# First attention of a Perceiver kernel: maxima and partial sums carried by transfers, divided by groups of four head pairs

## The reference

```
q = layernorm(x) @ Wq + bq            # 16 heads of width 16, scaled by 16 ** -0.5
k = ctx @ Wk + bk;  v = ctx @ Wv + bv # 2 batches x 4096 keys
o[h] = softmax(q[h] @ k[h].T) @ v[h]  # 32 (batch, head) products of 256 x 4096
x = x + concat(o) @ Wo + bo
```

## Time and profile before

| | |
|---|---|
| median of 3 runs | 1099.63 us (1094.17 to 1102.38) |
| profiled execution | 1102.66 us, its span 1101.4 us |
| first attention | 137.5 to 537.4 us of the span |
| TensorE busy over the span | 946.6 us (86%) |
| VectorE busy over the span | 822.6 us (75%) |
| ScalarE busy over the span | 650.5 us (59%) |
| GpSimd busy over the span | 299.6 us (27%) |
| mean granted clock of TensorE | 0.91 |

### The profile page before, as it was taken

One profiled execution on the slowest core, in us unless ns is written; L12 is line 12 of the kernel. 1 busy time (PEld: TensorE's weight loads), 2 busy tenths in 40 slices (PEclk: granted clock), 3 DMA queues, 4 the chain that ended last, 5 costly groups with the idle time before them and its releaser, 6 DMA issues. The chain is left out here.

```text
span 1101.4 us, 20954 instructions
## 1 busy us (share of the span) xinstructions
PE 946.6 (86%) x7732; PEld 589.9 (54%) x7732; DVE 822.6 (75%) x1712; ACT 650.5 (59%) x1045; POOL 299.6 (27%) x332
## 2 busy tenths in 40 slices
PE   6997859999999999998688996667887778799697
PEld 5886724444444444444365884643455556635455
DVE  5775777999999999992245987998877776278347
ACT  4442304888887878787354544249999999301212
POOL 1000088889800000000120552005555543000001
PEclk9998955999999999999799998776789999898989
DMA  6868651223323223310312216520165225770000
GB/s 215 307 226 281 243 143 39 76 76 80 82 76 81 74 75 82 82 45 1 76 43 87 79 37 160 132 64 1 43 167 152 58 58 171 217 203 8 0 0 20
DMA packets 99320, 111.83 MB, mean 102 GB/s; under 512 B 26658, under 2 KB 75730, under 8 KB 99218
## 3 DMA queue, kind: packets, MB, share of 16 engines
q1 hardware_dynamic: 98578, 109.89, 33.9%
q10 hardware_dynamic: 640, 0.59, 0.2%
HBM read 80.95 MB, written 29.43 MB: 100 GB/s over the span
## 5 line engine op out<-in xcount | busy, mean ns | idle before, releaser
L852 ACT ACTIVATE pT<-bank 128x512 f32<-128x512 f32 x512 | 278.4, 597 | 99.3 <-PE bank L769 78.7
L874 DVE TENSOR_REDUCE rmax<-bank 128x2 f32<-128x1024 f32 x256 | 307.3, 1223 | 32.3 <-PE bank L737 31.3
L781 PE MATMUL bank<-pT,V 128*17 128x256 f32 x2048 | 163.6, 392 | 4.7 <-ACT oT L858 4.6
L1755 PE MATMUL bank<-K1s,qs 97*128 97x512 f32 x256 | 112.7, 544 | 34.4 <-ACT work L1879 14.2
L769 PEld LDWEIGHTS bank<-qs,ks 49*128 49x128 f32 x1024 | 78.9, 189 | 114.9 <-ACT pT L852 101.3
L769 PE MATMUL bank<-qs,ks 49*128 49x256 f32 x1024 | 131.7, 336 | 2.3 <-ACT pT L852 0.5
L737 PE MATMUL bank<-ks,qs 49*128 49x512 f32 x512 | 111.9, 432 | 16.6 <-DMA ks<-k_parts_d 9.4
L2044 POOL TENSOR_TENSOR total<-total,work 128x1024 f32<-128x1024 f32 x40 | 94.9, 2379 | 32.9 <-ACT work L1879 32.0
L1755 PEld LDWEIGHTS bank<-K1s,qs 97*128 97x128 f32 x256 | 53.2, 219 | 51.8 <-issue 36.9
L1939 DVE MAX8 cand<-work 128x8 f32<-128x128 f32 x384 | 76.4, 277 | 0.0
L781 PEld LDWEIGHTS bank<-pT,V 128*17 128x17 f32 x2048 | 34.6, 95 | 64.3 <-ACT pT L852 41.7
(11 more groups left out here) (468 smaller groups left out, 1807.4 us busy)
## 6 DMA issues: line engine op xcount, KB each, us to landing
k_parts_d<-kparts SPq DMA_DIRECT2D x48, 512.0 KB
ks<-k_parts_d SPq DMA_DIRECT2D x381, 64.0 KB, 2.2
K1s<-k_parts_d SPq DMA_DIRECT2D x96, 128.0 KB
cn<-in_ctx SPq DMA_DIRECT2D x32, 384.0 KB, 3.5
cx<-in_ctx SPq DMA_DIRECT2D x16, 384.0 KB, 5.2
w<-in_L_ffn_w SPq DMA_DIRECT2D x32, 128.0 KB, 2.4
w2e<-in_L_ffn_w SPq DMA_DIRECT2D x16, 128.0 KB, 3.0
W<-in_L_xattn_W SPq DMA_DIRECT2D x2, 1024.0 KB, 7.8
```

The source lines that it names most:

```text
L781: t = pe.matmul(bank[32 * c:32 * c + VW, 7, a * S:(a + 1) * S], V[:, b * NCH + 4 * g + c, h, :], pT[:, (at + 2 * (c // 2) + a) % 8, c % 2 ...
L852: p_made.up(act.activation(pT[:, at % 8, :], bank[:, 4 + at % 3, :], ACT.Exp))
L874: max_read.up(dve.tensor_reduce(rmax[p % 2][:, :, qt, c], bank[:, b0:b0 + 2, :], AX.X, ALU.max))
L1755: m = pe.matmul(bank[:, b0 + c, :], qs1[0:NROW1, b * H1 + h, q], K1s[h][0:NROW1, keys], start=True, stop=(what == "new"))
```

## The change

The negated maxima no longer pass through TensorE: `move_rows(p)` on SP sends `nmax` (now 128 x 2 x 2) by four transfers of 128 elements into the row `MAX_ROW` of `qs`, and `scores(p, 0)` waits for these (`rows_in`). The sums no longer pass through TensorE either, but for the last pair: `move_parts(p)` on SP sends the four groups of `oT` by eight transfers into `parts` (the room of `xn`) and their sums into `den8`. `add_parts(k)` on GpSimd, behind its powers, adds the four parts of four pairs at once, VectorE takes the reciprocals of their sums in four pieces (`turn_den`), one after each of the maxima in steps 12 to 15 of pairs 4, 8 and 12 (`DEN_AT`), and `spread_den(k)` on SP spreads these by way of DRAM to `den16`; GpSimd multiplies. The last group holds three pairs, and pair 15 is added up by `add_quarters` at the end and divided by `divide_last`. The order of channels changes with it (the two heads of a pair are interleaved), so that `wo` is loaded in nine transfers instead of two, and the queries' high rows are interleaved so that a head's keys come in two transfers instead of three.

```diff
-    def steps_of(m, u):
-        return [(m, u)] + [(m - 1, "rows")] * (u == 0 and m > 0)
...
     def ahead(p, j):
         m, u = p + 1 + (j + LEAD) // 16, (j + LEAD) % 16
-        return steps_of(m, u) if m < NP_ else [(NP_ - 1, "rows")] * (m == NP_ and u == 0)
-
-    def beside(p, j):
-        return ahead(p, j) + [(p - 1, "sums")] * (j == 4 and p > 0)
-
-    passing = [what for u in range(16) for what in steps_of(0, u)]
-    passing += [what for u in range(LEAD) for what in steps_of(1, u)]
+        return [(m, u)] * (m < NP_)
+
+    passing = [(0, u) for u in range(16)] + [(1, u) for u in range(LEAD)]
+    DEN_AT = {}
     for p in range(NP_):
         for j in range(16):
-            passing += beside(p, j)
-    passing += [(NP_ - 1, "sums")]
+            passing += ahead(p, j)
+            if p % PG == 0 and p and j >= 12:
+                DEN_AT[len(passing) - 1] = (p // PG - 1, j - 12)
     place = {what: at for at, what in enumerate(passing)}
...
         powers_made.up(pool.tensor_scalar(Bp[1][:, :, :, :], Bp[1][:, :, :, :], -1.0, 0.0, ALU.mult, ALU.add))
         pool.wait_ge(*powers_made.at(1))
-        pool.wait_ge(*wo_in.at(32))
-        x_biased.up(pool.tensor_tensor(x[:, :, :], x[:, :, :], bob[:, :, :].to_broadcast([P, NT, D]), ALU.add))
+        for k in range(NG_):
+            add_parts(k)
+            if k == 0:
+                pool.wait_ge(*wo_in.at(16 * 9))
+                x_biased.up(pool.tensor_tensor(x[:, :, :], x[:, :, :], bob[:, :, :].to_broadcast([P, NT, D]), ALU.add))
+
+    def add_parts(k):
+        n, b, kt = pairs_of(k), k // 2, k % 2
+        r, h = slice(0, n * 2 * D0), slice(0, 2 * n)
+        for p in (PG * k + n - 2, PG * k + n - 1):
+            pool.wait_ge(*parts_in[p % 2].at(128 * (p // 2 + 1)))
+        den_added.up(pool.tensor_tensor(den8[h, 0:2, :], den8[h, 0:2, :], den8[h, 2:4, :], ALU.add))
+        pool.wait_ge(*den_added.at(2 * k + 1))
+        den_added.up(pool.tensor_tensor(den8[h, 0, :], den8[h, 0, :], den8[h, 1, :], ALU.add))
+        parts_added.up(pool.tensor_tensor(parts[r, 0:2, :], parts[r, 0:2, :], parts[r, 2:4, :], ALU.add))
+        pool.wait_ge(*parts_added.at(2 * k + 1))
+        parts_added.up(pool.tensor_tensor(parts[r, 0, :], parts[r, 0, :], parts[r, 1, :], ALU.add))
+        pool.wait_ge(*parts_added.at(2 * k + 2))
+        pool.wait_ge(*den_in.at(16 * (PG * k + n)))
+        ch_made.up(pool.tensor_tensor(xT[r, kt, b * S:(b + 1) * S], parts[r, 0, :], den16[r, :], ALU.mult))
...
-        for r0, kp, qp in STACK:
-            key_in[p % 2][q].up(queue.dma_start(ks[p % 2][HALF_P * a + r0:HALF_P * a + r0 + D0, cols].bitcast(F32),
-                                                k_parts_d[n * D0:(n + 1) * D0, kp, cols]), 16)
+        pairs = k_parts_d[n * D0:(n + 1) * D0, :, cols].rearrange("d s c -> (d s) c")
+        r0 = HALF_P * a
+        key_in[p % 2][q].up(queue.dma_start(ks[p % 2][r0:r0 + MAX_ROW, cols].bitcast(F32), pairs), 16)
+        key_in[p % 2][q].up(queue.dma_start(ks[p % 2][r0 + MAX_ROW + 1:r0 + NROW, cols].bitcast(F32),
+                                            k_parts_d[n * D0:(n + 1) * D0, 0, cols]), 16)
...
+        def move_rows(p):
+            sp.wait_ge(*nmax_made.at(p + 1))
+            for a in range(2):
+                for qt in range(2):
+                    r = HALF_P * a + MAX_ROW
+                    rows_in[p % 2].up(sp.dma_start(qs[p % 3][r:r + 1, qt * P:(qt + 1) * P].bitcast(F32),
+                                                   nmax[:, a, qt:qt + 1].bitcast(F32)), 16)
+
+        def move_parts(p):
+            sp.wait_ge(*oT_copied.at(p + 1))
+            if p % PG == 0 and p:
+                sp.wait_ge(*ch_made.at(p // PG))
+            i = p % PG
+            for c in range(4):
+                parts_in[p % 2].up(sp.dma_start(parts[2 * D0 * i:2 * D0 * (i + 1), c, :], oT[32 * c:32 * c + D0, :]), 16)
+                parts_in[p % 2].up(sp.dma_start(den8[2 * i:2 * i + 2, c, :], oT[32 * c + D0:32 * c + VW, :]), 16)
+
+        def spread_den(k):
+            n = pairs_of(k)
+            sp.wait_ge(*den_turned.at(4 * (k + 1)))
+            den_out.up(sp.dma_start(den8_d[0:2 * n, :], den8[0:2 * n, 1, :]), 16)
+            sp.wait_ge(*den_out.at(16 * (k + 1)))
+            for i in range(n):
+                den_in.up(sp.dma_start(den16[2 * D0 * i:2 * D0 * (i + 1), :], den8_d[2 * i:2 * i + 2, :]
+                                       .rearrange("(o a) n -> o a n", o=1).to_broadcast([D0, 2, S])), 16)
+
+        load_queries(2)
+        move_rows(0)
+        for p in range(NP_):
+            if p:
+                move_parts(p - 1)
             for q in range(4):
-                load_keys(p, q)
+                if p + 2 < NP_:
+                    load_keys(p + 2, q)
+                if q == 1 and p + 1 < NP_:
+                    move_rows(p + 1)
+            if p + 3 < NP_:
+                load_queries(p + 3)
+            if p and p % PG == 0:
+                spread_den(p // PG - 1)
+        spread_den(NG_ - 1)
...
-        def turn_rows(p):
-            at = place[p, "rows"]
-            pe.wait_ge(*nmax_made.at(p + 1))
-            pe.wait_ge(*max_read.at(at - 1))
-            for qt in range(2):
-                t = pe.transpose(bank[:, 2 * (at % 2), qt * P:(qt + 1) * P], nmax[:, qt, :], ident[:, :])
-            max_made.up(t)
-
-        def add_quarters(p):
-            at = place[p, "sums"]
-            pe.wait_ge(*oT_copied.at(p + 1))
-            pe.wait_ge(*max_read.at(at - 1))
+        def add_quarters():
+            pe.wait_ge(*fold_made.at(16))
+            pe.wait_ge(*oT_copied.at(NP_))
             for a in range(2):
-                for qt in range(2):
-                    t = pe.matmul(bank[:, 2 * (at % 2), (2 * a + qt) * 32:(2 * a + qt) * 32 + VW],
-                                  oT[:, a * S + qt * P:a * S + (qt + 1) * P], fold[:, :], start=True, stop=True)
-            max_made.up(t)
+                for n in range(2):
+                    r = slice(LAST_ROW - 32 * n, LAST_ROW - 32 * n + 2 * D0)
+                    t = pe.matmul(bank[r, n, 0:S], fold[:, n, a, :, :].rearrange("p d a -> p (d a)"), oT[:, a * S:(a + 1) * S],
+                                  start=(a == 0), stop=(a == 1))
+            fold_summed.up(t)
 
         def scores(p, j):
...
             if j == 0:
-                pe.wait_ge(*max_read.at(place[p, "rows"] + 1))
+                pe.wait_ge(*rows_in[p % 2].at(64 * (p // 2 + 1)))
...
+        def project(i, kt):
+            return pe.matmul(bank[:, 2 + i % 2, i // 2 * D:(i // 2 + 1) * D], xT[:, kt, i * P:(i + 1) * P], wo[:, kt, :],
+                             start=(kt == 0), stop=(kt == 1))
+
+        def project_first():
+            pe.wait_ge(*wo_in.at(16 * 9))
+            pe.wait_ge(*max_read.at(len(passing)))
+            pe.wait_ge(*ch_made.at(2))
+            for i in range(2):
+                project(i, 0)
+                proj_made.up(project(i, 1))
+
+        def project_last():
...
                 for what in ahead(p, j):
-                    pass_on(*what)
-                if j == 4 and p:
-                    add_quarters(p - 1)
+                    max_step(*what)
                 weigh_half(16 * p + j)
-                if p == NP_ - 1 and j == 6:
-                    turn_batch(0)
                 if p == NP_ - 1 and j == 9:
-                    project_batch(0)
+                    project_first()
         for step in range(16 * NP_, 16 * NP_ + 2):
             weigh_half(step)
-        add_quarters(NP_ - 1)
-        turn_batch(1)
-        project_batch(1)
+        add_quarters()
+        project_last()
...
         def sum_out(p):
             act.wait_ge(*pv_made.at(16 * (p + 1)))
             if p:
-                act.wait_ge(*max_made.at(place[p - 1, "sums"] + 1))
+                act.wait_ge(*parts_in[(p - 1) % 2].at(128 * ((p - 1) // 2 + 1)))
             oT_copied.up(act.copy(oT[:, :], bank[:, 7, :]))
...
             if u == 15:
                 dve.wait_ge(*max_read.at(at + 1))
-                nmax_made.up(dve.tensor_reduce(nmax[:, :, :].rearrange("p t (a m) -> p a t m", a=2)[:, :, :, MAX_ROW],
-                                               rmax[p % 2][:, :, :, :], AX.X, ALU.max, negate=True))
-
-        def copy_rows(p):
-            at = place[p, "rows"]
-            dve.wait_ge(*max_made.at(at + 1))
+                if p:
+                    dve.wait_ge(*rows_in[(p - 1) % 2].at(64 * ((p - 1) // 2 + 1)))
+                nmax_made.up(dve.tensor_reduce(nmax[:, :, :], rmax[p % 2][:, :, :, :], AX.X, ALU.max, negate=True))
+
+        def turn_den(k, part):
+            h, q = slice(0, 2 * pairs_of(k)), slice(part * S // 4, (part + 1) * S // 4)
+            dve.wait_ge(*den_added.at(2 * k + 2))
+            den_turned.up(dve.reciprocal(den8[h, 1, q], den8[h, 0, q]))
+
+        def divide_last(qt):
+            r, q = slice(LAST_ROW, P), slice(qt * P, (qt + 1) * P)
```

(81 more changed lines are left out.)

81 lines of the change are left out of this document (29 added, 52 removed).

## The result

| kernel | median of its runs, us | lowest to highest | ratio to before, 95% interval |
|---|---|---|---|
| before | 1099.63 | 1094.17 to 1102.38 | |
| changed | 1123.42 | 1115.34 to 1130.43 | 1.0224 (1.0188 to 1.0259) |

Slower by 2.2%, beyond the range of 1096 to 1114. The profiled execution of the changed kernel was the shortest of its five, 1115.34 us (span 1114.0). The first attention ends in it at 553.43 us against 537.44 in the earlier trace rows, 16.0 us later; what follows takes 560.6 us against 564.0.

A forecast was written before the change was run, and what follows sets the result against it. Bound: the TensorE-ScalarE loop and two detours through the maxima's banks. Terms 17.6 - 22.6 + 6.4 + 2.0 + 0.6 = +4.0 us, giving 1103.6 against the median of 1099.63; range 1096 to 1114.

The forecast's parts named there:

- Term 1: Pair 4: VectorE stands for 27 us until GpSimd, behind its powers, raises `den_added` 2; +17.6 us at TensorE's maximum (6,4).
- Term 2: From the stall to the phase's end: pairs without both rotations, a shorter last pair and tail; -22.6 us.
- Term 3: After the stall: TensorE resumes at 1.2 GHz for 15 us, 7 steps of 0.92; +6.4 us (1.7 to 8.3).
- Term 4: Reciprocals of groups 1 and 2: four consecutive VectorE steps of 1.69 against 1.222 us; +2.0 us (0 to 3.7).
- Term 5: Rows by DMA: hidden in most pairs, SP late from `spread_den` at pairs 5, 9, 13; +0.6 us (0 to 5).
- row against rule: Rows of 128 4-byte elements: by the skill's rule the stage's dearest transfers; `gcol`, similarly cut up, took 4.3 us to land.
- Rival B: Rows land late in each of ten pairs, 7 to 12 us, more behind `spread_den`; about 1115 us, 17%.
- rival D: VectorE doesn't stand at pair 4, GpSimd having finished its powers before; 1072 us, 5%.

The follow-up runs named there:

- the second profile of before: The kernel before, unchanged, profiled once more in a single run: 1097.6 us, end of the phase at 535.76.
- the kernel with the rows alone: The kernel before with `move_rows` and without `turn_rows` and `copy_rows`, sums left in the rotation: 1090.68 us, ratio 0.9941.
- the one with the keys first: The changed kernel, with SyncE loading quarter 0 of the keys before the parts in pairs 5, 9 and 13: 1101.77 us, ratio 1.0022.
- the second profile: The changed kernel, unchanged, run once more: profiled execution 1124.6 us, median 1127.4 us.
- the second measurement: The changed kernel, unchanged, measured once more against the kernel before: 1127.4 us, ratio 1.0272.
- the kernel with both edits: The changed kernel, with GpSimd's first-group sums inside its chain of powers and quarter 0 of keys before parts in pairs 5, 9, 13: 1071.24 us, ratio 0.9763.

## Why the prediction was wrong

- **Term 1** (+17.6) held. den_added 2 was put at 298.96 and came at 299.91: the chain of powers ended at 297.79 and not 296.74 (the second profile of before has 297.92, so the change is not behind it), the additions took 1.25 and 0.71 us where 1.30 and 0.75 were put, on 8 partitions as on 128. TensorE went on at 301.71 instead of 300.9, so +18.4.
- **Term 2** (-22.6) measured -25.3: pairs of 19.98 against 19.91 forecast, and the kernel with the rows alone gives the two shares, 0.76 and 1.22. The end, from the last `nmax` to the next phase, gave 5.5 us (39.73 to 34.24) where 2.3 were put.
- **Term 3** (+6.4) stayed in its range. The earlier trace rows has 0.50 until 188 and 0.96 behind it, so the return that the prediction puts between 186 and 188 was at 188, and its 15 us were nearer 16. From the stall to `nmax` 7 the first profile lost 4.4 (53.27 - 30.33 - 19.98 = 2.96, and 1.45 in the next pair, 1.22 of them the wait for keys in pair 5), the second 5.6, and the one with the keys first 7.4 (57.71 - 30.33 - 19.98), where 1.2 GHz lasted until 320.7.
- **Term 4** (+2.0) measured 0.5: 20.21 for a pair with reciprocals. The error is the step of 1.69 us: behind on its banks, VectorE takes 1.08 us a maximum and not 1.137 (300.42 to 301.50 in the rows above is one), and a maximum with a reciprocal took 1.55 (299.95 to 301.50). The seven maxima that follow the reciprocals of group 1 then stand 1.08 to 1.14 apart until the step is 1.22 again, which makes up part of the rest; four in a row, 1.7 us at once, cost 0.8.
- **Term 5** (+0.6, at most 5) is the step that failed. It measured +17.0: 7.6 between `nmax` 10 and 11, 9.4 between 14 and 15 (6.7 and 11.2 in the second profile). Its sentence "SP comes late from `spread_den`" is right, the order of its queue too; but it asked only when the rows are due, at 20.9. The same list puts the keys of quarter 0 behind the parts, from 12.5 to 14.4, so landed at 16.6, and `max_step`(p+2, 0) wants them in step 11 of the same pair, at 11 x 1.222 + 0.36 = 13.8. A wait of 2.8 us stood in the numbers of the prediction, unread. In pair 9, from its first scores at 387.21, the parts began at 10.3 and not 9.3, their eight issues took 5.2 us and not 3.2 (0.65 each in place of 0.4), the keys took 2.6 to land and not 2.2, and the maximum was due some 0.7 later: that made it 5.0. Half clock behind it cost 2.6 and 4.5 more. Nor did pair 5 hide it in slow steps in the first profile: 1.2 us.
- The half clock is priced by its length. A step takes 2.14 us at 0.50 (409.02 to 411.16 for the maxima of pair 9) against 1.222, so each us at 1.2 GHz loses 0.43. Behind the keys' waits of the two profiles TensorE worked 5.5, 10.0, 3.9 and 16.5 us so, which gives 2.4, 4.3, 1.7 and 7.1; the pairs, less the wait and 19.98, lost 2.6, 4.5, 1.9 and 6.9.
- The terms as measured, 18.4 - 25.3 + 4.4 + 0.5 + 17.0, add up to 15.0 of the 16.0 us; 1 us has no owner. Without the 17.0 the phase would have ended 1.0 us before that of the kernel before; the prediction without Term 5 has 3.4 behind it. With 17.0 in the place of 0.6 its own sum gives 1120.0 us.
- The rows landed in 2.0 us, though each is cut into 128 elements, less than the keys' 2.6, so the dear transfer of the paragraph on row against rule didn't appear. The profile puts 1.4 us in three places down to them, all of it at weight loads, none at a matmul. But behind `spread_den` they were in time only because the keys were later still. They went out at 19.2 in pair 9, not 16.2, and landed at about 23 (an estimate: the last of four issues begins at 408.2, and 2.0 to landing), where the prediction has the need at 20.9. With the keys first, they cost TensorE 0.65 and 0.60 us. Rival B named a slower outcome with the wrong transfer; its 1115 is not a hit.
- The profiles give +18 us for the phase (554.5 against 536.6), the medians +24 and +28 for the whole. The part behind the phase explains some 2 of the difference, which leaves 4 to 8. The granted clock of each execution accounts for most of the rest. The changed kernel's nine executions with a clock on record go from a span of 1114.0 us at a mean of 0.896 to 1129.8 at 0.878; with two levels, 0.50 and 1.00, that is 232 and 276 us at 1.2 GHz. Between the medians of the second measurement the changed kernel has 71 us more at 1.2 GHz than the kernel before, between the means of the profiles 54. The other 17, at 0.43, are 7 of the 8 us. Where in the execution they lie is not recorded. They needn't lie behind the waits: the kernel before has no such waits in its phase, and nineteen runs of it spread by 12 us all the same, from 1092.81 us at 0.922 to 1104.95 at 0.909.

Forecast by its own rival D, no stall, were 1072 us; the kernel with both edits took 1071.2. The agreement is partly luck: D had the reciprocals at 3 us, the last pair and the end at 2.4, and no wait for keys, and by the profiles the phase is 33 us shorter and not 28. The saving of the change is real, and two placements hid it.

## What to carry to other kernels

When an edit gives a queue more to do, go through everything that stands behind the new entries, with the moment at which each is due, not only through what the edit itself adds: loads that run two stages ahead are due earlier than their name says. A wait on an engine with long work of its own (GpSimd's chain) is settled by moving the small operation into that work, which cost nothing that these runs show (the chain of powers ended 6 us later, and nothing waited for it). And where TensorE is at full clock, price a wait with what follows it: 2 us idle made a pair 6 us longer, while VectorE's absence for 1.8 us with two banks in hand cost 0.8 and no clock.
